# The last image of an attention and bilinear layer kernel: another order of work behind the last attention, and a second buffer for one left-over chunk

## The reference

```
x = x + gamma * attention(group_norm(x))        # queries and keys of 32 channels, softmax over 4096 points
y = relu(bn(w1 @ group_norm(x)))                # 256 -> 32 channels
z = relu(bn(w2 @ [y_i * y_j for all i >= j]))   # 528 products -> 256 channels
x = x + z
```

## Time and profile before

| | |
|---|---|
| median of 3 runs | 2377.39 us (2374.01 to 2380.53) |
| the profiled execution | 2370.43 us |
| its span, first to last instruction | 2368.6 us |
| mean granted TensorE clock | 0.988 of 2.4 GHz |
| TensorE, VectorE, ScalarE, GpSimd busy | 95%, 80%, 71%, 27% of the span |

### The profile page before, as it was taken

One profiled execution on the slowest core, in us unless ns is written; L12 is line 12 of the kernel. 1 busy time (PEld: TensorE's weight loads), 2 busy tenths in 40 slices (PEclk: granted clock), 3 DMA queues, 4 the chain that ended last, 5 costly groups with the idle time before them and its releaser, 6 DMA issues. The chain is left out here.

```text
span 2368.6 us, 42584 instructions
## 1 busy us (share of the span) xinstructions
PE 2242.1 (95%) x16782; PEld 1641.4 (69%) x16782; DVE 1902.4 (80%) x3133; ACT 1669.9 (71%) x2691; POOL 627.7 (27%) x608
## 2 busy tenths in 40 slices
PE   2899999999999999999899999999899999999977
PEld 1577777776777777777677777777677777777722
DVE  6878888877788888887788888888778777778676
ACT  3477777776677777777577777777677777777754
POOL 2100111111222333232522133233322222222243
PEclk9999999999999999999999999999999999999989
DMA  4000000000012221221122212222101111111101
GB/s 171 22 1 1 1 8 8 8 16 1 10 51 59 68 66 53 66 57 37 37 55 59 65 46 59 57 63 57 37 14 42 34 33 33 33 28 33 33 32 54
DMA packets 56664, 95.22 MB, mean 40 GB/s; under 512 B 8016, under 2 KB 14864, under 8 KB 56464
## 3 DMA queue, kind: packets, MB, share of 16 engines
q1 hardware_dynamic: 56464, 92.49, 13.8%
HBM read 67.03 MB, written 19.14 MB: 36 GB/s over the span
## 5 line engine op out<-in xcount | busy, mean ns | idle before, releaser
L1014 ACT ACTIVATE ph<-sps,esc 128x512 f16<-128x512 f32 x1024 | 703.7, 687 | 409.5 <-PE sps L1240 403.5
L1367 PE MATMUL acc<-hth,ph 128*128 128x257 f16 x4096 | 958.7, 274 | 6.4 <-ACT ot L1020 6.4
L1368 PE MATMUL acc<-htl,ph 128*128 128x256 f16 x4096 | 957.6, 274 | 0.0
L615 DVE TENSOR_REDUCE mx<-tps 128x1 f32<-128x512 f32 x1024 | 702.1, 687 | 316.6 <-PE tps L1224 312.8
L634 DVE TENSOR_TENSOR pl<-p,ph 128x512 f16<-128x512 f32 x1024 | 813.7, 795 | 42.2 <-ACT p L1015 41.3
L1015 ACT ACTIVATE p<-sps,esc 128x512 f32<-128x512 f32 x1024 | 699.4, 683 | 0.0
L1372 PE MATMUL acc<-hth,pl 128*128 128x257 f16 x4096 | 622.5, 274 | 0.0
L1372 PEld LDWEIGHTS acc<-hth,pl 128*128 128x128 f16 x4096 | 400.8, 98 | 160.6 <-issue 1.7
L1368 PEld LDWEIGHTS acc<-htl,ph 128*128 128x128 f16 x4096 | 401.7, 98 | 151.3 <-issue 1.4
L1367 PEld LDWEIGHTS acc<-hth,ph 128*128 128x128 f16 x4096 | 401.9, 98 | 79.5 <-issue 9.2
L863 POOL TENSOR_TENSOR xl<-xn,xh 128x512 f16<-128x512 f32 x176 | 226.9, 1311 | 849.1 <-DVE xn L585 847.2
(11 more groups left out here) (212 smaller groups left out, 1639.7 us busy)
## 6 DMA issues: line engine op xcount, KB each, us to landing
rt<-turned SPq DMA_DIRECT2D x96, 256.0 KB, 4.3
xt<-x SPq DMA_DIRECT2D x36, 512.0 KB, 3.7
xb<-x SPq DMA_DIRECT2D x32, 512.0 KB, 5.0
out<-zt SPq DMA_DIRECT2D x48, 256.0 KB, 2.1
rt<-turned SPq DMA_DIRECT2D x72, 64.0 KB, 4.7
turned<-yb SPq DMA_DIRECT2D x24, 96.0 KB, 1.9
out<-fst SPq DMA_DIRECT2D x8, 256.0 KB, 2.0
out<-htl SPq DMA_DIRECT2D x8, 256.0 KB, 2.0
```

The source lines that it names most:

```text
L615: V.reduce_max(mx[:, tile, c:c + 1], tps[par][:], AX).then_inc(t_free[par], 1)
L1014: A(ph[:, u % SLOTS], sps[u % 2][:], ACT.Exp, scale=esc[:]).then_inc(ph_ok, 1)
L1367: mm(acc[j][:, 0:C + 1], w, hth[:, t], start=(t == 0), stop=False)
L1368: mm(acc[j][:, 0:C], w, htl[:, t], start=False, stop=False)
```

## The change

Behind the last attention, and in the loop over the last image's chunks:

- VectorE makes the low half of y of the chunk after next behind the fourth product of the next chunk, where it had made that of the next chunk behind all of its products. The 32-bit normalized values move among the first products in a like way.
- TensorE issues each selecting matmul one group ahead: behind the `pairs` of group g it turns group g + 1 of chunk n + 1, and behind the fifth it turns group 0 of chunk n + 2.
- z's second half of the left-over chunk 23 goes to `p32[:, 0]` instead of `zt0`, and ScalarE takes both halves out ahead of the first y.
- For the last chunk TensorE makes the whole first output half and then the second, and VectorE, with a semaphore of its own, adds x to the second half.

```diff
+        def z_half(n, h):
+            if n >= SHARED:
+                return zt[set_of(n)][:, h]
+            return p32[:, 0] if n == SHARED - 1 and h else zt0[:]
...
             def store(n, h):
...
+                if n == B * NCH - 1 and h:
+                    sp.wait_ge(res_dve, 1)
...
         # VectorE
             bias(second_norm(LASTB), 1)
+            dve.wait_ge(gn_ok, second_norm(LASTB) + 1)
+            normed(("second", LASTB, 0))
             product_low(SHARED - 1, 4)
-            dve.wait_ge(gn_ok, second_norm(LASTB) + 1)
-            for c in range(2):
-                normed(("second", LASTB, c))
+            normed(("second", LASTB, 1))
             halves_low(SHARED)
+            product(SHARED, 0)
+            product(SHARED, 1)
+            product_low(SHARED, 0)
             normed(("second", LASTB, 2))
-            product(SHARED, 0)
-            for grp in range(1, 5):
+            for grp in range(2, 5):
                 product(SHARED, grp)
                 product_low(SHARED, grp - 1)
+            halves_low(SHARED + 1)
             product_low(SHARED, 4)
-            for c in range(NCH):
+            for c in range(NCH - 1):
                 n = SHARED + c
-                if c + 1 < NCH:
-                    halves_low(n + 1)
-                    product(n + 1, 0)
+                product(n + 1, 0)
                 if c + 3 < NCH:
                     normed(("second", LASTB, c + 3))
-                if c + 1 < NCH:
-                    for grp in range(1, 5):
-                        product(n + 1, grp)
-                        product_low(n + 1, grp - 1)
-                    product_low(n + 1, 4)
+                for grp in range(1, 5):
+                    product(n + 1, grp)
+                    product_low(n + 1, grp - 1)
+                    if grp == 3 and c + 2 < NCH:
+                        halves_low(n + 2)
+                product_low(n + 1, 4)
+            dve.wait_ge(z_ok, 2 * B * NCH)
+            o = z_half(B * NCH - 1, 1)
+            V.tensor_tensor(o, o, xb[LASTB % 2][:, 1, HW - CH:HW], ALU.add).then_inc(res_dve, 1)
...
         # ScalarE
             for c in range(2):
                 high(("second", LASTB, c))
+            for h in range(H2):
+                z_out(SHARED - 1, h, acc[2 + h])
             y_out(SHARED, tps[0])
             halves_high(SHARED)
+            product_high(SHARED, 0)
             high(("second", LASTB, 2))
-            for h in range(H2):
-                z_out(SHARED - 1, h, acc[2 + h])
-            product_high(SHARED, 0)
+            product_high(SHARED, 1)
             y_out(SHARED + 1, tps[0])
             halves_high(SHARED + 1)
-            for grp in range(1, 5):
+            for grp in range(2, 5):
                 product_high(SHARED, grp)
...
         # TensorE
                 if c == 0:
-                    for grp in range(3):
+                    for grp in range(2):
                         turned_channels(n, grp)
-            for grp in range(3, 5):
+            for grp in range(2, 5):
                 turned_channels(SHARED, grp)
+            turned_channels(SHARED + 1, 0)
             for c in range(NCH):
                 n = SHARED + c
                 pe.wait_ge(z_ok, 2 * (n - 1))
+                if c + 1 == NCH:
+                    for h in range(H2):
+                        for grp in range(5):
+                            pairs(n, h, grp, acc[2 * (c % 2) + h])
+                    break
                 for grp in range(5):
                     for h in range(H2):
                         pairs(n, h, grp, acc[2 * (c % 2) + h])
-                    if c + 1 < NCH:
-                        turned_channels(n + 1, grp)
+                    if grp < 4:
+                        turned_channels(n + 1, grp + 1)
                     if c + 2 < NCH and grp == 1:
...
+                if c + 2 < NCH:
+                    turned_channels(n + 2, 0)
```

More of the change, by code:

```diff
@@ L184, in build @@
         z_mm, z_ok = sem("z_mm"), sem("z_ok")
-        res_ok = sem("res_ok")
+        res_ok, res_dve = sem("res_ok"), sem("res_dve")
         og_free = sem("og_free")
@@ L352, in store @@
                 b, c = divmod(n, NCH)
[L353 to L356, removed]
-                else:
-                    sp.dma_start(dst, zt[set_of(n)][:, h]).then_inc(og_last[set_of(n)], 16)
+                if n == B * NCH - 1 and h:
+                    sp.wait_ge(res_dve, 1)
+                else:
+                    sp.wait_ge(res_ok, 2 * n + h + 1)
+                sp.dma_start(ov[b, :, h, c * CH:(c + 1) * CH],
+                             z_half(n, h)).then_inc(og_free if n < SHARED else og_last[set_of(n)], 16)
             for c in range(NCH):
@@ L899, in residual @@
                 pool.wait_ge(z_ok, 2 * n + h + 1)
-                o = zt0[:] if n < SHARED else zt[set_of(n)][:, h]
+                o = z_half(n, h)
                 tt(o, o, xb[b % 2][:, h, c * CH:(c + 1) * CH], ALU.add).then_inc(res_ok, 1)
@@ L947, in _ @@
                     low(("second", LASTB, c + 3))
-                for h in range(H2):
+                for h in range(H2 if c + 1 < NCH else 1):
                     residual(SHARED + c, h)
@@ L1044, in z_out @@
                 act.wait_ge(z_mm, 2 * n + h + 1)
[L1045 to L1053, removed]
+                if n >= SHARED + 2:
+                    act.wait_ge(og_last[set_of(n)], 32 * ((n - SHARED) // 2))
+                elif 0 < 2 * n + h < 2 * SHARED - 1:
+                    act.wait_ge(og_free, 16 * (2 * n + h))
+                A(z_half(n, h), bank[:], ACT.Relu, bias=t2[:, h:h + 1], scale=sc2[:, h:h + 1]).then_inc(z_ok, 1)
             def project():
```

## The result

The changed kernel ran in 2357.35 us (median of 4 runs, 2354.99 to 2358.98) against 2375.70 for the kernel before, measured again (4 runs, 2372.66 to 2380.53): ratio 0.992, 95% interval 0.990 to 0.994. That is 18.35 us less, where 14.2 were forecast, and 0.15 us under the low end of the range. The profiled execution took 2357.45 us, its span is 2354.6, where the prediction had 2354.4. So the profile shows the forecast to 0.2 us, and the median is 5.85 us under the forecast one. That is the question of the experiments.

What follows compares the result with a forecast made beforehand. No single bound: TensorE stalled 1.79 us per chunk for VectorE's late low half of y, after which VectorE would bound. Gains 3.4 + 3.6 + 1.8 + 3.8 + 1.6 = 14.2 took 2377.39 to 2363.2 us; range 2357.5 to 2370.

Steps and rivals of the forecast that it cites:

- Low stretches: Times when TensorE runs at 1.2 GHz: forecast to cost 1.6 us each, with one expected in chunk 24.
- T1: Start of chunk 25's first w2 matmul on TensorE: forecast at 2286.4 against 2289.82, a gain of 3.4 us.
- T0: Start of chunk 24's first w2 matmul on TensorE: forecast at 2275.7, 3.4 us later, waiting for chunk 25's y.
- chunk 24: From T0 to T1, without its stall: 9.1 us plus 1.6 for low clock, 10.7 where 17.55 stood.
- chunks 25 to 28: Steady chunks with normalizing: 10.4 us each, 41.6 against 45.23, a gain of 3.6.
- chunk 29: Chunk with nothing left to normalize, so TensorE bounds it: 9.1 us, a gain of 1.8.
- chunk 30: Chunk without stall, low clock or a selecting matmul behind it: 7.4 us against 11.20, a gain of 3.8.
- T7 to the end: Chunk 31, from its first w2 matmul on TensorE to the end: 9.8 us against 11.44, a gain of 1.6.
- VectorE as the bound: In chunks 25 to 28, with the stall gone, VectorE rather than TensorE sets the time: 10.4 us a chunk.
- the blocking that was added for it: In chunks 25 to 28, one more VectorE instruction blocked by GpSimd per chunk, taken as 0.8 us.
- The rival "TensorE bounds": Chunks 25 to 28 take 9.1 to 9.6 us each, a total gain of 17.4 to 19.4; chance 10%.
- The clock: TensorE's clock: low once in chunk 24, no later drop; rival, it keeps falling, median 2369.6 or 2365 to 2366; chance 17%.

Runs made afterwards that it cites:

- the second profile of before: The kernel before run once more with no edit: 2373.50 us (11 runs) against 2374.64, ratio 0.9993.
- the kernel with only the buffer: Kernel before, with only chunk 23's second z half in its own buffer and both halves taken out ahead of the first y: 2375.59 us, one run.
- the stall of 2.33: TensorE's stall in the changed kernel with the low half of y put back behind the last product's low half: 2378.62 us, one run.

## Why the prediction was wrong, and where it was right

**The step that failed** is the one from the profile to the runs: "The sum is made against the profiled execution: 2370.43 us ... The median of the runs, 2377.39, is 6.96 above it", and then "the median to **2363.2 us**". It took the 6.96 for something that stays. In the changed kernel the profiled execution lay 0.1 above the median of its four runs instead. The median of three runs was itself high: over 44 runs the kernel before takes 2374.27, 3.1 less, and over 15 the changed one 2358.98, 1.6 more than its first four said. From 2374.27 the forecast 14.2 would have given 2360.1, 1.1 from the pooled result.

**The range** failed with it. Its low end, 2357.5, was the base less the largest gain of a rival (2377.39 - 19.4 = 2358.0), and its upper end, 2370, the base less a gain just over 7. The spread of the runs, 6.5 us, was named, but neither end was moved by more than half a us for it.

**Where the spread lies**: ahead of the change. The 13 profiles start their tails between 2254.6 and 2263.3, whichever kernel it is, and the tail itself repeats: 114.0 and 114.3 before, 99.3, 99.1 and 100.8 after. This is read from profiled executions; for the runs without a profile it is inferred. What makes the 2255 us ahead vary was not tried; it stays open. Low stretches in the last image, the first theory, play a part of 1.6 us each: the second profile of before had three, not two. They don't explain the spread, which for the changed kernel, with no low stretch behind T1 in any of its three profiles, is 15 us (2352.17 to 2367.21).

**The terms of the sum**, in the profile:

| | forecast | measured |
|---|---|---|
| T0, against the kernel before | 3.4 later | 3.9 later, 0.7 of it ahead of the tail |
| chunk 24 | 10.7 | 10.71 |
| T1 | gain 3.4 | 2.97, 3.7 in the tail |
| chunks 25 to 28 | 4 x 10.4 | 41.55 |
| chunk 29 | 9.1 | 9.06 |
| chunk 30 | 7.4 | 7.46 |
| T7 to the end | 9.8 | 9.68 |
| all, span | 14.2 | 14.0, 14.7 in the tail |

That the span came within 0.2 us is in part luck. In the two profiles of the kernel before, chunk 24 differs by 1.2 us and T1 to T7 by 1.6; in the three of the changed kernel, the time to T1 differs by 1.8 (31.30 to 33.06).

**VectorE as the bound** held, and so did the size of the blocking that was added for it (0.7 us instead of 0.8), though it came from two more blocked instructions and not from one. Without GpSimd's adds a chunk takes 9.4, and with the normalized values off VectorE 9.15, which is TensorE's own time. The rival "TensorE bounds" came true only there. The Trainium skill (SBUF — State Buffer, "Who interferes with whom") gave 10.2 to 10.8 by an exclusive lock; the trace agrees, at 10.4. The words that the prediction quotes, "fully blocks", the page has for VectorE's 2-port modes; of an instruction with two SBUF inputs it says that it contends. The normalizing instruction, on which the prediction showed the lock, reads one tensor beside its per-channel factors. The prediction's reading of it, the rest of GpSimd's 1.25 us and then a whole 0.54, is also off by 0.24: GpSimd's record ends at 2317.18, and VectorE's, of 1.56, ends 0.30 later. Beside GpSimd's adds of x the two normalizing instructions took 2.36 and GpSimd's adds 2.68 instead of 2.48.

**The clock** recovered as forecast: one low stretch in chunk 24, none behind it. The waits left, 1.17 to 1.30 us in each of four chunks, brought none. Between T1 and T7 the stall of 1.79 was followed by a low stretch in two of six chunks, in the second profile of before in three of six, and in the kernel with only the buffer in two of six; the stall of 2.33 four times of five. The Trainium skill (TensorE: Matmul & The Clock Gate, "HAM oscillation — how this bites in real kernels") tells of a kernel in which TensorE waits about 3 to 5 us for a transfer ahead of each burst of matmuls and starts every burst at the low clock. The trace agrees for a wait of that order: behind the 6.03 us ahead of T0 a selecting matmul takes 0.60 us, where the last single one ahead of the wait took 0.39. The page's example is no guide for the waits of 1.2 to 2.3 us here; for those only the counts above stand.

## What to carry to other kernels

A forecast of a few us is to be checked, and made, against a fixed place in the profile just ahead of the change, and turned into a run's time with the spread of the runs on both sides: a gap between one profile and the median of three runs is noise until it repeats. In a list written by hand, look for the instruction at the end of one stage that belongs to the next; moving it can gain what stands between, while moving only what reads it made this kernel slower. When a stall goes, add up what each engine is busy for including its blocked time: the next bound is there, and work of a third engine can be what fills it.

## What was not expected of the hardware

A short stall can cost TensorE more than itself: 56 matmuls on constants, in the place of 1.79 us of waiting per chunk, made the kernel 3.1 to 7.6 us faster. With VectorE and GpSimd both adding at the same time at the end, VectorE's add took 1.19 us instead of 0.69. And an instruction on 32 partitions is held like one on 128: the low half of y took 1.80 us instead of 0.68 beside GpSimd's add.
